# Seven rows of every four gathers, fetched by SyncE one at a time

## The chip, the cores and the metric

The kernel runs on 1 core of one Trainium2 chip. The metric is the device time of one execution in microseconds (us); the figure quoted is the median of three executions. A profile of one more execution gives the span from its first to its last instruction.

## The reference, cut to what matters

The reference is one layer of a graph network over 6250 nodes (128 features: 32 scalars and 32 vectors of three components) and 200,000 edges, sorted by receiving node (`dst`).

```python
h = relu(layernorm(x))                       # nodes
s, v = h[:, :32] @ W_up_s, h[:, 32:] x W_up_v  # the node table, 128 numbers a node
w = silu(silu(edge_feats @ A1 + b1) @ A2 + b2) @ A3   # 4 x 32 weights an edge
ss, vs = s[src], v[src]                      # one gathered row of the table an edge
out_s0 = ss * y_s * w0
out_s3 = sum_i(vs_i * y_v_i) / sqrt(3) * w3
out_v1 = ss * y_v * w1
out_v2 = vs * y_s * w2
message = segment_sum(concat(...), dst) / 10
out = x + (message x W_out)
```

## The kernel before

**First stage.** TensorE, ScalarE, VectorE and GpSimd compute the node table, 6272 rows of 512 bytes, in about 40 us, and SyncE stores it to HBM (`node_table`). Semaphore `table_stored` says that it is there.

**Edge stage.** The edges are padded and cut into tiles of 128 edges, one edge on each partition. Four tiles are a quad, four quads (16 tiles) a block, two blocks one iteration of the loop. There are NJ = 49 iterations; the last is written out after the loop and has fewer tiles. So a loop of 48 iterations does 96 blocks, or 384 quads, and the last iteration the rest (1563 tiles in all).

- **GpSimd (POOL), lines 519 to 543.** `gather(j, p)` waits, at the first quad of a block, for the block's sender numbers (`src_loaded`), then for the rows slot of the quad to be free (`msgs_ready`: the quad that used the slot one iteration ago has been consumed), and issues four indirect DMAs. Each reads 128 sender numbers, one on each partition of `src_in`, and fetches 128 rows of the table into `rows`. All four raise `gathered[p]`. There are eight slots, one for each quad of an iteration.
- **TensorE** computes the edge weights in three layers and, in `scatter`, multiplies each quad's messages by a one-hot matrix to sum them by receiving node in windows of 32 nodes.
- **VectorE** waits in `messages(j, p)` for `gathered[p]`, for the edge weights and for a messages slot, and multiplies rows by weights (lines 653 and 655). It also makes the one-hot matrices and adds the finished windows (`add_window`, which loads the window's start, one number, from SBUF into a register, line 663).
- **SyncE (SP), lines 482 to 515,** loads the inputs of blocks. In the loop, for each of the two blocks: it waits until the last quad of the block has been gathered, issues the load of the sender numbers of the same block of the next iteration (`load_src`, line 495), waits for layer 1 (`l1_done`), issues the edge features (line 486), waits for the one-hot matrices (`onehot_ready`), and issues the edge attributes and receivers (lines 491 and 492). Everything on SP runs in the order in which it is written.

The order of work on each engine is the order of the program; engines meet at semaphores alone.

Of the kernel before, what the change touches and what calls it, by code (L numbers as in the profile page):

```python
# [22 lines left out]
F32, I32 = mybir.dt.float32, mybir.dt.int32  # L23
ALU, ACT, AX = mybir.AluOpType, mybir.ActivationFunctionType, mybir.AxisListType

P = 128
# [6 lines left out]
NPAD = NT * P  # L33
CT = 7
NCH = NT // CT
PIECES = [(0, 4), (4, 3)]

GROUP = 2 * P
QT = 4
QUADS = 4  # L40
OW = QT
TILES = QT * QUADS
BLOCK = TILES * P
BODY = 2
QB = BODY * QUADS
NJ = -(-N_EDGES // (BLOCK * BODY))
NB = NJ * BODY
# [4 lines left out]
GP = 112  # L52
XW = NPAD + W
MAX_ROUNDS = NPAD // W + 1
SLOTS = 2
MSG_SLOTS = 4
HOT_SLOTS = 4
# [23 lines left out]
def quad_tiles(p):  # L81

    o, half = divmod(p, 2)
    begins = [o * OCT_EDGES + w * GROUP + half * P for w in range(OW)]
    return sum(b < LAST_EDGES for b in begins)


def gnn_layer_kernel(nc, x, xT, src, dst, dst_groups, attr, efT, Wus, Wuv, A1, b1, A2, b2, A3, Wos, Wov, outT):
    table = nc.dram_tensor("node_table", (NPAD, F), F32, kind="Internal").ap()
# [4 lines left out]
    with ctx:  # L94
        def sb(name, shape, dt=F32):
            return ctx.enter_context(nc.sbuf_tensor(name, shape, dt))
# [4 lines left out]
        def sem(name):  # L101
            return ctx.enter_context(nc.semaphore(name))
# [35 lines left out]
        rows = sb("rows", [P, QT * QB, F])  # L138
# [7 lines left out]
        ef_in = sb("ef_in", [2 * EF, BODY, 2 * MLP_HALF])  # L146
        attr_in = sb("attr_in", [P, BODY, TILES * 4])
        dst_in = sb("dst_in", [P, BODY, TILES], I32)
        src_in = sb("src_in", [P, BODY, TILES], I32)

        x_sb = sb("x_sb", [P, NT, F])
        tab_sb = sb("tab_sb", [P, NT, F])
# [37 lines left out]
        table_stored = sem("table_stored")  # L190
# [7 lines left out]
        round_step = sem("round_step")  # L198
        ef_loaded = [sem(f"ef_loaded{b}") for b in range(BODY)]
        attr_loaded = [sem(f"attr_loaded{b}") for b in range(BODY)]  # L200
        src_loaded = [sem(f"src_loaded{b}") for b in range(BODY)]
        gathered = [sem(f"gathered{p}") for p in range(QB)]
        src_again = sem("src_again")
        slots_claimed = sem("slots_claimed")
        l1_done = sem("l1_done")
        h1_ready = sem("h1_ready")
        l2_done = sem("l2_done")
        h2_ready = sem("h2_ready")
        w_ready = sem("w_ready")
        msgs_ready = sem("msgs_ready")  # L210
# [9 lines left out]

        out_stored = sem("out_stored")

        round_sems = [round_step, *ef_loaded, *attr_loaded, *src_loaded, *gathered, src_again, slots_claimed, l1_done, h1_ready, l2_done,
                      h2_ready, w_ready, msgs_ready, rel_ready, eq_ready, onehot_ready, scatter_done, sums_copied, sums_turned, turned_copied, out_ready,
                      window_added]

# [1 line left out]
        with nc.Block() as block:  # L228
# [154 lines left out]
            def _(dve):  # L383
# [28 lines left out]
                def count_rounds():  # L412
# [8 lines left out]
                    dve.wait_ge(rounds_step, 4)  # L421
                    dve.tensor_scalar(rounds_sb[:, :], span_windows[:, :], 1.0, float(MAX_ROUNDS),
                                      ALU.add, ALU.min).then_inc(rounds_step, 1)
# [56 lines left out]
        with nc.Fori(0, rounds):  # L480
            with nc.Block() as block:

                @block.sync
                def _(sp):
                    def load_ef(j, b):
                        sp.dma_start(ef_in[:, b, :], efT[bass.ds(j * BODY + b, 1), :, :].rearrange("a p n -> (a p) n")
                                     ).then_inc(ef_loaded[b], 16)

                    def load_attr(j, b):
                        n = bass.ds(j * BODY + b, 1)  # L490
                        sp.dma_start(attr_in[:, b, :], attr[n, :, :].rearrange("a p n -> (a p) n")).then_inc(attr_loaded[b], 16)
                        sp.dma_start(dst_in[:, b, :], dst[n, :, :].rearrange("a p n -> (a p) n")).then_inc(attr_loaded[b], 16)

                    def load_src(j, b):
                        sp.dma_start(src_in[:, b, :], src[bass.ds(j * BODY + b, 1), :, :].rearrange("a p n -> (a p) n")
                                     ).then_inc(src_loaded[b], 16)

                    for b in range(BODY):
                        sp.sem_inc(src_loaded[b], SRC_CREDIT)
                    for b in range(BODY):  # L500
                        load_ef(0, b)
                        load_attr(0, b)
                    with sp.Fori(0, NJ - 1) as j:
                        for b in range(BODY):
                            sp.wait_ge(gathered[b * QUADS + QUADS - 1], j * 16 * QT + 16 * QT)
                            load_src(j + 1, b)
                            sp.wait_ge(l1_done, j * 2 * BODY + 2 * b + 2)
                            load_ef(j + 1, b)
                            sp.wait_ge(onehot_ready, j * 2 * BODY + 2 * b + 2)
                            load_attr(j + 1, b)  # L510
                    for p in range(QB):
                        sp.wait_ge(gathered[p], (NJ - 1) * 16 * QT + 16 * quad_tiles(p))
                    for b in range(BODY):
                        sp.dma_start(src_in[:, b, :], src[b, :, :]).then_inc(src_again, 16)
                    sp.wait_ge(src_again, 16 * BODY)

                @block.gpsimd
                def _(pool):
                    pool.wait_ge(table_stored, 16 * NCH * len(PIECES))

                    def gather(j, p, tiles=QT):
                        b, k = divmod(p, QUADS)
                        if k == 0:
                            pool.wait_ge(src_loaded[b], j * 16 + 16)
                        pool.wait_ge(msgs_ready, j * QB + p + 1)  # L525

                        pool.sem_inc(slots_claimed, 1)  # L527
                        for t in range(tiles):
                            at = QT * k + t
                            pool.indirect_dma_start(  # L530
                                out=rows[:, QT * p + t, :], out_offset=None, in_=table,
                                in_offset=bass.IndirectOffsetOnAxis(ap=src_in[:, b, at:at + 1], axis=0),
                            ).then_inc(gathered[p], 16)

                    with pool.Fori(0, NJ - 1) as j:  # L535
                        for p in range(QB):
                            gather(j, p)

                    for p in range(QB):
                        gather(NJ - 1, p, quad_tiles(p))  # L540
                    for p in range(QB):
                        pool.wait_ge(gathered[p], (NJ - 1) * 16 * QT + 16 * quad_tiles(p))

                    pool.dma_reset()
# [60 lines left out]
                def _(dve):  # L605
# [36 lines left out]
                            .unsqueeze(3).broadcast_to([P, HT, 4, W]),  # L642
                            ALU.mult).then_inc(onehot_ready, 1)

                    def messages(j, p, tiles):

                        dve.wait_ge(gathered[p], j * 16 * QT + 16 * tiles)
                        dve.wait_ge(w_ready, j * QB + p + 1 + W_CREDIT)
                        dve.wait_ge(scatter_done, j * QB + p + 1)
                        g = rows[:, QT * p:QT * (p + 1), :].rearrange("p t (c u) -> p t c u", c=4)  # L650
                        m = msgs[:, p % MSG_SLOTS].rearrange("p t k (c u) -> p t k c u", c=4)
                        w = psw[:, p % SLOTS]
                        dve.tensor_tensor(m[:, :, :, 0, :], g[:, :, 0, :].unsqueeze(2).broadcast_to([P, QT, 2, MUL]),  # L653
                                          w[:, :, :, 0, :], ALU.mult)
                        dve.tensor_tensor(m[:, :, :, 1:4, :],  # L655
                                          g[:, :, 1:4, :].unsqueeze(2).broadcast_to([P, QT, 2, 3, MUL]),
                                          w[:, :, :, 1, :].unsqueeze(3).broadcast_to([P, QT, 2, 3, MUL]),
                                          ALU.mult).then_inc(msgs_ready, 1)
# [14 lines left out]
                    def iteration(j, first=False, last=False):  # L673
                        for p in range(QB):


                            g = p // 2 + 1
                            ahead = (j + g // 4, g % 4) if not (last and 2 * g >= QB) else None
                            n = 2 * p - WINDOW_LAG
                            if p % 2 == 0 and not (first and n < 0):  # L680
                                for i in range(OW):
                                    add_window(j, n + i)
                            messages(j, p, quad_tiles(p) if last else QT)
                            if ahead and p % 2 == 0:
                                relative(*ahead)
                                equal(*ahead)
                            elif ahead:
                                scale(*ahead)
# [5 lines left out]
                    with dve.Fori(1, NJ - 1) as j:  # L694
                        iteration(j)
# [164 lines left out]
```

## Time and profile before

| | us |
|---|---|
| time, median of 3 executions | 2016.88 (2015.19 to 2016.98) |
| time of the profiled execution | 2015.93 |
| its span, first to last instruction | 2014.1 |
| POOL busy | 1491.1 |
| TensorE matmuls busy | 1544.4 |
| VectorE busy | 977.5 |
| ScalarE busy | 418.5 |

The profile does not count instructions of an engine's queue as busy: register arithmetic, semaphores, branches and the issuing of DMAs by SP are shown with a q behind the engine's name (SPq, DVEq). Idle time that ends with "issue" is time in which the engine waited for nothing that the profile shows.

### The profile page before, as it was taken

How to read it: one execution, taken by the hardware profiler on the slowest of the kernel's cores; microseconds unless marked ns; L12 is line 12 of the kernel's file. 1: busy time of each engine (PE TensorE's matmuls, PEld its weight loads, DVE VectorE, ACT ScalarE, POOL GpSimd, SP SyncE). 2: the span in 40 equal slices, each digit the busy share in tenths (PEclk: the TensorE clock that was granted, in tenths of full speed). 3: DMA queues.
4: the chain of work that ended last, by engine and by line, in shares of the span. 5: the costliest groups of instructions: out<-in, count | busy, mean ns of one | idle time of the engine just before them, and what ended most of it. 6: DMA issues, size and time to landing. Idle time of an engine off the chain costs nothing.

```text
span 2014.1 us, 47833 instructions
## 1 busy us (share of the span) xinstructions
PE 1544.4 (77%) x16198; PEld 942.1 (47%) x16198; DVE 977.5 (49%) x2232; ACT 418.5 (21%) x836; POOL 1491.1 (74%) x1627
## 2 busy tenths in 40 slices
PE   6887787886877778868768787787777887776875
PEld 3444454454544545535445455454444454444543
DVE  4444444444444444444444444444444444444443
ACT  4222222222221222222222122222222222222121
POOL 4777777777777777777777777777777777777774
PEclk8888889789888897898898878988889789789787
DMA  8222222222222222222222222222222222222222
GB/s 230 58 61 57 59 58 59 57 60 57 59 58 59 57 60 58 57 60 57 59 58 59 57 60 57 59 58 59 57 60 57 59 58 59 57 60 57 59 58 100
DMA packets 111252, 128.24 MB, mean 64 GB/s; under 512 B 70786, under 2 KB 83362, under 8 KB 111108
## 3 DMA queue, kind: packets, MB, share of 16 engines
q0 software_dynamic: 50336, 102.64, 19.7%
q1 hardware_dynamic: 60324, 25.34, 4.8%
q8 instruction: 9, 0.15, 0.0%
q10 hardware_dynamic: 576, 0.05, 0.0%
q14 instruction: 7, 0.06, 0.0%
HBM read 121.47 MB, written 6.43 MB: 64 GB/s over the span
## 4 chain that ended last, share of the span: by engine, by line
POOL 71%; issue 25%; POOLq 1%; DMA 1%; PE 1%; SPq 1%; DVE 0%; ACT 0%; DVEq 0%; ACTq 0%
POOL rows L530 71%; DMA x_sb<-in_x 1%; POOLq L525 1%; POOLq L527 0%; POOLq L535 0%; SPq L246 0%; DMA node_table<-tab_sb 0%; SPq L236 0%; PE pss L750 0%; DVE bn L388 0%; DMA rows<-node_table,src_in 0%; PE psw L728 0%; DVE group_stats L439 0%; PE psw L456 0%; SPq L240 0%
## 5 line engine op out<-in xcount | busy, mean ns | idle before, releaser
L530 POOL DMA_INDIRECT rows<-node_table,src_in x1563 | 1475.3, 944 | 486.6 <-issue 486.6
L750 PE MATMUL pss<-msgs,onehot 128*32 128x64 f32 (+1 forms) x12544 | 336.1, 254 | 432.2 <-DVE msgs L655 430.6
L750 PEld LDWEIGHTS pss<-msgs,onehot 128*32 128x32 f32 x12544 | 264.3, 120 | 676.4 <-DVE msgs L655 659.3
L728 PE MATMUL psw<-a_bd,h 128*128 128x256 f32 x1568 | 564.4, 494 | 3.4
L653 DVE TENSOR_TENSOR msgs<-rows,psw 128x256 f32<-128x256 f32 x392 | 165.0, 421 | 797.6 <-DMA rows<-node_table,src_in 787.6
L655 DVE TENSOR_TENSOR msgs<-rows,psw 128x768 f32<-128x768 f32 x392 | 371.3, 947 | 0.0
L728 PEld LDWEIGHTS psw<-a_bd,h 128*128 128x128 f32 x1568 | 326.8, 231 | 86.2 <-issue 25.9
L565 ACT ACTIVATE h<-ps,b_sb 128x512 f32<-128x512 f32 x196 | 134.8, 688 | 996.7 <-PE ps L718 996.7
L712 PE MATMUL ps<-ef_in,a_bd 16*128 16x512 f32 x392 | 241.7, 698 | 12.1 <-DMA ef_in<-in_efT 10.4
L718 PE MATMUL ps<-h,a_bd 128*128 128x512 f32 x392 | 246.5, 716 | 0.9 <-ACT h L565 0.9
L671 DVE TENSOR_TENSOR xT_sb<-xT_sb,psx 128x32 f32 x784 | 145.9, 186 | 199.9 <-DVE xT_sb L671 157.3
L638 DVE TENSOR_TENSOR onehot<-psx,attr_in 128x1024 f32<-128x1024 f32 x196 | 238.7, 1218 | 0.0
L558 ACT ACTIVATE h<-ps,b_sb 128x512 f32<-128x512 f32 x196 | 134.7, 687 | 370.0 <-PE ps L712 370.0
L769 PEld LDWEIGHTS psx<-sums_t,w_out 128*128 128x128 f32 x784 | 168.9, 265 | 25.8 <-ACT sums_t L577 0.7
L769 PE MATMUL psx<-sums_t,w_out 128*128 128x128 f32 x784 | 161.0, 343 | 0.5 <-ACT sums_t L577 0.5
L761 PEld LDWEIGHTS psx<-identity,sums 128*128 128x128 f32 x392 | 41.4, 148 | 166.2 <-DVE xT_sb L671 89.4
L571 ACT ACTIVATE sums<-pss 128x256 f32<-128x256 f32 x196 | 75.3, 384 | 187.5 <-PE pss L750 164.0
L712 PEld LDWEIGHTS ps<-ef_in,a_bd 16*128 16x128 f32 x392 | 62.4, 198 | 86.8 <-issue 76.0
L761 PE MATMUL psx<-identity,sums 128*128 128x128 f32 x392 | 91.2, 317 | 1.9 <-ACT sums L571 1.1
L629 DVE TENSOR_TENSOR psx<-psx,rel 128x256 f32<-128x256 f32 x196 | 84.7, 432 | 6.8
L718 PEld LDWEIGHTS ps<-h,a_bd 128*128 128x128 f32 x392 | 78.6, 248 | 4.0 <-issue 3.9
L577 ACT ACTIVATE sums_t<-psx 128x256 f32<-128x256 f32 x196 | 73.9, 377 | 4.9 <-PE psx L761 4.9
(60 smaller groups left out, 138.5 us busy)
## 6 DMA issues: line engine op xcount, KB each, us to landing
rows<-node_table,src_in POOLq DMA_INDIRECT x1563
ef_in<-in_efT SPq DMA_DIRECT2D x98, 64.0 KB
xT_sb<-in_xT SPq DMA_DIRECT2D x7, 448.0 KB, 8.2
x_sb<-in_x SPq DMA_DIRECT2D x7, 448.0 KB, 7.4
attr_in<-in_attr SPq DMA_DIRECT2D x98, 32.0 KB
out_T<-xT_sb SPq DMA_DIRECT2D x1, 3136.0 KB, 8.8
node_table<-tab_sb SPq DMA_DIRECT2D x7, 256.0 KB, 3.9
src_in<-in_src SPq DMA_DIRECT2D x100, 8.0 KB, 1.6
```

The source lines that it names most:

```text
L530: pool.indirect_dma_start(out=rows[:, QT * p + t, :], out_offset=None, in_=table, in_offset=bass.IndirectOffsetOnAxis(ap=src_in[:, b, at:a ...
L558: act.activation(h1[:, o % 2, :], ps1[:, 0, :], ACT.Silu, bias=b1_sb[:, 0:1]).then_inc(h1_ready, 1)
L565: act.activation(h2[:, b, h, :], ps2[:, 0, :], ACT.Silu, bias=b2_sb[:, 0:1]).then_inc(h2_ready, 1)
L638: dve.tensor_tensor(onehot[:, g, :, :, :], eq.unsqueeze(2).broadcast_to([P, HT, 4, W]), attr_in[:, b, h * 4 * HT:(h + 1) * 4 * HT].rearran ...
L653: dve.tensor_tensor(m[:, :, :, 0, :], g[:, :, 0, :].unsqueeze(2).broadcast_to([P, QT, 2, MUL]), w[:, :, :, 0, :], ALU.mult)
L655: dve.tensor_tensor(m[:, :, :, 1:4, :], g[:, :, 1:4, :].unsqueeze(2).broadcast_to([P, QT, 2, 3, MUL]), w[:, :, :, 1, :].unsqueeze(3).broad ...
L671: dve.tensor_tensor(at, at, pso[:, i * W:(i + 1) * W], ALU.add).then_inc(window_added, 1)
L712: nc.tensor.matmul(ps1[:, 0, :], a1_bd[:, :], ef_in[:, b, h * MLP_HALF:(h + 1) * MLP_HALF], start=True, stop=True).then_inc(l1_done, 1)
L718: nc.tensor.matmul(ps2[:, 0, :], a2_bd[:, :], h1[:, o % 2, :], start=True, stop=True).then_inc(l2_done, 1)
L728: last = nc.tensor.matmul(psw[:, p % SLOTS, 2 * i:2 * i + 2].rearrange("p b c d e -> p (b c d e)"), h2[:, b, h, (2 * half + i) * P:(2 * ha ...
L750: last = nc.tensor.matmul(to, onehot[:, o, QT * half + w, c, :], moving, start=(half == 0 and c == 0), stop=(half == 1 and c == 3), skip_g ...
L769: last = nc.tensor.matmul(pso, w_out[:, k, :], sums_t[:, o % 2, k, :], start=(k == 0), stop=(k == 1))
```

## The change

GpSimd's four gathers of a quad fetch 128, 127, 126 and 124 rows, always from partition 0 on. The seven rows left over (one, two and four, on the last partitions) are fetched by SyncE, one plain DMA of 512 bytes each, whose source address comes from a register. For this the host appends the 28 sender numbers of a block's left-over edges to `src_in` (44 columns on each partition where there were 16), and SyncE loads the 28 numbers from partition 0 into registers at the head of each block, then waits at each quad for its slot. VectorE's `messages` waits for the seven single rows as well. The first wait of SyncE on the table (`table_stored`) is new. The last iteration, outside the loop, gathers full tiles as before.

```diff
+GATHER_ROWS = [P, P - 1, P - 2, P - 4]
+LEFT_OVER = [(t, e) for t, n in enumerate(GATHER_ROWS) for e in range(n, P)]
+SINGLES = len(LEFT_OVER)
+SRC_COLS = TILES + QUADS * SINGLES
...
-        src_in = sb("src_in", [P, BODY, TILES], I32)
+        src_in = sb("src_in", [P, BODY, SRC_COLS], I32)
...
+                    def gather_singles(j, b):
+
+                        sp.wait_ge(src_loaded[b], j * 16 + 16)
+                        sp.sem_inc(singles_claimed, 1)
+                        nodes = nc.values_load_multi_w_load_instructions(
+                            src_in[0:1, b, TILES:SRC_COLS], engines=[mybir.EngineType.SP], min_val=0, max_val=NPAD - 1,
+                            skip_runtime_bounds_check_because="the senders are node numbers")[1]
+                        for k in range(QUADS):
+                            p = b * QUADS + k
+                            sp.wait_ge(msgs_ready, j * QB + p + 1)
+                            sp.sem_inc(singles_claimed, 1)
+                            for (t, e), node in zip(LEFT_OVER, nodes[k * SINGLES:(k + 1) * SINGLES]):
+                                sp.dma_start(rows[e:e + 1, QT * p + t, :], table[bass.ds(node, 1), :]
+                                             ).then_inc(singles_gathered[p], 16)
+
...
+                    sp.wait_ge(table_stored, 16 * NCH * len(PIECES))
                     with sp.Fori(0, NJ - 1) as j:
                         for b in range(BODY):
+                            gather_singles(j, b)
                             sp.wait_ge(gathered[b * QUADS + QUADS - 1], j * 16 * QT + 16 * QT)
...
-                    def gather(j, p, tiles=QT):
+                    def gather(j, p, tiles=QT, last=False):
...
+                            n = P if last else GATHER_ROWS[t]
                             pool.indirect_dma_start(
-                                out=rows[:, QT * p + t, :], out_offset=None, in_=table,
-                                in_offset=bass.IndirectOffsetOnAxis(ap=src_in[:, b, at:at + 1], axis=0),
+                                out=rows[0:n, QT * p + t, :], out_offset=None, in_=table,
+                                in_offset=bass.IndirectOffsetOnAxis(ap=src_in[0:n, b, at:at + 1], axis=0),
                             ).then_inc(gathered[p], 16)
...
-                    def messages(j, p, tiles):
+                    def messages(j, p, tiles, last):
 
                         dve.wait_ge(gathered[p], j * 16 * QT + 16 * tiles)
+                        if not last:
+                            dve.wait_ge(singles_gathered[p], j * 16 * SINGLES + 16 * SINGLES)
```

## Rows read from the trace of the kernel before

**Rows 1.** The page: busy time by engine, and the chain that ended last by engine.
```profile
PE 1544.4 (77%) x16198; PEld 942.1 (47%) x16198; DVE 977.5 (49%) x2232; ACT 418.5 (21%) x836; POOL 1491.1 (74%) x1627
...
POOL 71%; issue 25%; POOLq 1%; DMA 1%; PE 1%; SPq 1%; DVE 0%; ACT 0%; DVEq 0%; ACTq 0%
```

**Rows 2.** The page's groups: instruction, count, busy us, mean ns, idle before, releaser.
```profile
L530 POOL DMA_INDIRECT rows<-node_table,src_in x1563 | 1475.3, 944 | 486.6 <-issue 486.6
...
L653 DVE TENSOR_TENSOR msgs<-rows,psw 128x256 f32<-128x256 f32 x392 | 165.0, 421 | 797.6 <-DMA rows<-node_table,src_in 787.6
```

**Rows 3.** Timeline of POOL from 1000 us: start us, duration us, what, idle before.
```profile
1001.70 0.94 POOL L530 DMA_INDIRECT rows<-node_table,src_in  x1 [0.30 <-issue]
1002.95 0.94 POOL L530 DMA_INDIRECT rows<-node_table,src_in  x1 [0.31 <-issue]
```

**Rows 4.** Waits of SP's queue: waiter, releaser, us in total, times, longest.
```profile
SPq L495 <- DMA rows<-node_table,src_in: 1690.3, 96, 21.0
```

**Rows 5.** Timeline of SP from 1003 us, one block to the next.
```profile
1003.17 0.33 SPq L495 DMA_DIRECT2D src_in<-in_src  x1
1003.79 0.33 SPq L486 DMA_DIRECT2D ef_in<-in_efT  x1
1004.31 0.33 SPq L491 DMA_DIRECT2D attr_in<-in_attr  x1
1004.87 0.33 SPq L492 DMA_DIRECT2D dst_in<-in_dst  x1
1023.14 0.33 SPq L495 DMA_DIRECT2D src_in<-in_src  x1
```

**Rows 6.** Timeline of SP near 32 us: loads to one partition, then one to 128.
```profile
31.92 0.29 SPq L256 DMA_DIRECT2D span_row<-window_spans  x1
32.25 0.23 SPq L257 DMA_DIRECT2D start_row<-window_starts  x1
32.53 0.35 SPq L258 DMA_DIRECT2D start_all<-window_starts  x1
```

**Rows 7.** SP's lines 486, 491, 503, 499: durations ns min/median/max, first and last start.
```profile
L486 SPq DMA_DIRECT2D ef_in<-in_efT x98: 331/331/429, 40.9 to 1962.7; - x98
L486 SPq FUSED_REGOPS  x96: 37/40/43, 65.4 to 1962.5; - x96
L486 SPq MOVE ef_in<-in_efT x96: 29/29/29, 65.5 to 1962.6; - x96
L491 SPq DMA_DIRECT2D attr_in<-in_attr x98: 332/336/423, 41.3 to 1963.2; - x98
L503 SPq MOVE  x1: 29/29/29, 43.7 to 43.7; - x1
L499 SPq EVENT_SEMAPHORE  x2: 17/17/17, 40.8 to 40.9; - x2
```

**Rows 8.** VectorE's queue, lines 663 and 694: register load of one number, register arithmetic.
```profile
L663 DVEq TENSOR_LOAD <-start_at x784: 297/303/330, 64.8 to 2003.2; - x196
L663 DVEq FUSED_REGOPS  x658: 46/55/71, 85.1 to 1955.4; - x165
L694 DVEq FUSED_REGOPS  x47: 98/98/104, 84.3 to 1922.5; - x47
```

**Rows 9.** Groups by line: plain DMAs issued by POOL, of 8 rows, then 64 rows.
```profile
L279 POOL DMA_DIRECT2D a_bd<-in_A x2 | 1.3, 656 | 0.1
L281 POOL DMA_DIRECT2D a_bd<-in_A x2 | 1.1, 551 | 0.0
```

**Rows 10.** The page: packets and bytes of the gathers' queue, share of 16 engines' span.
```profile
q0 software_dynamic: 50336, 102.64, 19.7%
```

**Rows 11.** Stretches of 20 us: PE, PEld, DVE, ACT, POOL busy, granted clock, DMA share, GB/s.
```profile
1000.00:1020.00 20.00, 12.81 (x178) 7.71 (x170) 9.73 (x22) 4.07 (x8) 15.12 (x17) 1.00 0.23 58
1040.00:1060.00 20.00, 17.20 (x172) 9.89 (x168) 9.75 (x23) 4.09 (x8) 15.12 (x17) 0.76 0.23 58
```

**Rows 12.** Timeline of the end: last load of senders, last gather, last window.
```profile
1962.03 0.33 SPq L495 DMA_DIRECT2D src_in<-in_src  x1
1993.06 0.94 POOL L530 DMA_INDIRECT rows<-node_table,src_in  x1 [0.30 <-issue]
2003.63 0.19 DVE L671 TENSOR_TENSOR xT_sb<-xT_sb,psx 128x32 f32 x1 [0.28 <-DVE xT_sb L671]
```

More of the change, by code:

```diff
@@ L203, in gnn_layer_kernel @@
         src_again = sem("src_again")
+        singles_gathered = [sem(f"singles_gathered{p}") for p in range(QB)]
         slots_claimed = sem("slots_claimed")
+        singles_claimed = sem("singles_claimed")
         l1_done = sem("l1_done")
@@ L221, in gnn_layer_kernel @@
         out_stored = sem("out_stored")
-        round_sems = [round_step, *ef_loaded, *attr_loaded, *src_loaded, *gathered, src_again, slots_claimed, l1_done, h1_ready, l2_done,
+        round_sems = [round_step, *ef_loaded, *attr_loaded, *src_loaded, *gathered, src_again, *singles_gathered, slots_claimed, singles_claimed, l1_done, h1_ready, l2_done,
                       h2_ready, w_ready, msgs_ready, rel_ready, eq_ready, onehot_ready, scatter_done, sums_copied, sums_turned, turned_copied, out_ready,
@@ L539, in _ @@
                     for p in range(QB):
-                        gather(NJ - 1, p, quad_tiles(p))
+                        gather(NJ - 1, p, quad_tiles(p), last=True)
                     for p in range(QB):
@@ L682, in iteration @@
                                     add_window(j, n + i)
-                            messages(j, p, quad_tiles(p) if last else QT)
+                            messages(j, p, quad_tiles(p) if last else QT, last)
                             if ahead and p % 2 == 0:
@@ L830 @@
     tiles = lambda a: np.ascontiguousarray(octs(a).reshape(NB, TILES, P, -1).transpose(0, 2, 1, 3).reshape(NB, P, -1))
+    senders = tiles(np.pad(src, (0, pad)))
+    singles = np.stack([senders[:, e, QT * k + t] for k in range(QUADS) for t, e in LEFT_OVER], axis=1)
     arrays = {
@@ L833 @@
         "xT": np.ascontiguousarray(x_pad[:, FEATURES].T),
-        "src": tiles(np.pad(src, (0, pad))),
+        "src": np.concatenate([senders, np.broadcast_to(singles[:, None, :], (NB, P, QUADS * SINGLES))], axis=2),
         "dst": tiles(dst_pad),
```

## The prediction

> **What bounds the kernel now.** I read the page's busy line and chain first. TensorE has the most busy time, but the chain that ended last is 71% POOL and 25% "issue" [rows 1], and the groups say that both are one line: 1563 gathers of 944 ns, with 486.6 us of "issue" between them, while VectorE's 797.6 us of idle time before the messages are ended by gathers landing [rows 2]. The timeline shows the pattern: a gather starts every 1.25 us, 0.94 of it busy and 0.30 between, whatever the other engines do [rows 3]. A block of 16 gathers so takes 19.97 us, the distance of SP's two `load_src` [rows 5]. The other engines have room: TensorE is busy for 12.8 to 17.2 us of a block (by its granted clock), VectorE for 9.7 [rows 11]. SP is nearly idle: it spends 1690.3 us waiting for gathers, 17.6 us in each of 96 blocks [rows 4]; its four loads of a block take 1003.17 to 1005.20 us [rows 5].
>
> So only two things in this change can move the time: what a gather costs POOL when it has a few rows less, and whether what SP gets to do fits in a block of 19.97 us.
>
> **POOL's side.** 96 blocks lose 28 rows each. The trace has only full gathers, so the price of a row is bounded. Above: if all 944 ns were per row, a row is 7.4 ns and a quad saves 52 ns, over 384 quads 20 us [rows 2]. At the other end: a plain DMA of 8 rows took POOL 656 ns and one of 64 rows 551 ns, so rows there cost nothing or less than nothing [rows 9]. I take zero, the nearest row about row counts, and keep -20 us. That a count that is no multiple of 16 makes a gather dearer can't be excluded by these rows (the 8-row DMA was the slower one, by 105 ns); three such gathers a quad at 105 ns more would be 0.32 us a quad, 121 us in all.
>
> **SP's side, by block.** What is added: 28 numbers loaded into registers, 28 DMAs each with its address arithmetic, five semaphore increments and five waits.
>
> *One single row.* A load with an address from a register is, on SP, a FUSED_REGOPS of 40 ns, a MOVE of 29 ns and the DMA instruction [rows 7]. The DMA instruction took 0.33 us for 16 or 128 partitions, with a register address or without [rows 5, 7]; the nearest to a single row is the load to one partition, 0.23 us when nothing was waited for [rows 6]. Between queue instructions lie about 0.04 us: 32.25 + 0.23 to 32.53 is 0.05 [rows 6]. Sum: (0.04 + 0.03 + 0.23) + 3 x 0.04 = 0.42 us; 28 of them 11.8 us. Bounds: 0.34 without the arithmetic (9.5 us) and 0.54 with a DMA of 0.33, two rounded gaps included (15.1 us).
>
> *The 28 register loads.* The trace has only a load of one number, on VectorE's queue: 303 ns [rows 8]. The low end is one instruction for all at the price of one, 0.35 us. The high end is one instruction, or its full price, for each: 28 x 0.34 = 9.5 us. I take the fixed part of an instruction off and pay the rest for each number, since the sequencer has to fetch each: register arithmetic there costs 55 to 98 ns [rows 8], which leaves 0.205 to 0.248 a number; with the mean, 28 x 0.226 + 0.08 = 6.4 us.
>
> The Trainium skill ("Runtime: NRT & Kernel Launch", section "Instruction fetch mechanics") says that a register load costs some 200 ns a register even in bulk. The 303 ns row, one register with its fixed part, agrees with that. By the page alone the 28 would be an estimated 5.6 us and the block 0.8 us shorter than below, an estimated 77 us less in all. It is the rule that speaks against this change: loading many numbers at once doesn't make them cheap.
>
> *The rest.* Five increments and up to five waits at 17 ns and a gap each [rows 7]: 0.6 us. The loads SP did before: 2.03 us, with the wait's own arithmetic ahead and half of the loop's branch some 2.4 us [rows 5, 7].
>
> Sum S = 11.8 + 6.4 + 0.6 + 2.4 = 21.2 us against 19.97. The bounds are 12.6 and 27.6.
>
> **What follows when S is over a block.** SP does everything in order. Behind the 28 DMAs stands `load_src` for the same block of the next iteration, and POOL's first gather there waits for it. While SP is early this wait is free: POOL needs the numbers one block later. When SP takes S > 20, POOL catches up with SP and waits for `src_loaded` at each block, and the period of the whole loop becomes S. The gathers' 4.97 us a quad stop being the bound.
>
> The total: SP's loop starts at 43.7 us [rows 7] and makes 96 turns; then come SP's last `load_src`, and behind it the 11 gathers of the final block (13.7 us), since POOL has by then finished the block before, the load's own issue and landing, some 2.3 us, and the 21.0 us from the last gather's start to the span's end [rows 12]. So span = 43.7 + 96 S + 37 = 81 + 96 S. At S = 21.2 it is 2116 us, and with the 1.8 us by which the profiled execution's time exceeds its span, 2118. The profiled execution was 1.0 us below the median. The change loses 102 us by this. It begins to lose at S = 20.1; below that the POOL path stands, as the wait before `load_src` had 17.6 us of room [rows 4].
>
> **What else is late, and doesn't decide.** SP starts the singles of a block only when the block before has been gathered. So VectorE's first quad of a block waits about 2.4 + 6.4 + 3 + 2 us, some 14 us, where gathers alone would let it go after 5 + 1.6; the quads behind come at 7 x 0.42 = 2.9 us. VectorE and TensorE catch up within the block (9.7 and at most 17.2 us of work [rows 11]), and the slot that POOL wants is eight quads, 40 us, old. No cost in the sum. The new waits on `msgs_ready` are met for the same reason; the wait for `table_stored` was POOL's anyway. `src_in` grows by 14 KB a block: nothing beside a queue at 19.7% [rows 10].
>
> **Rival 1, the SP work fits (S under 20.1): chance 0.30.** For it: the register load may be pipelined; two of the four terms have their low ends far down. The sum stays POOL's: 2016 less 0 to 20 us. Half of it or more would be faster by over 0.2%, if the rows cost anything. About 2008.
>
> **Rival 2, a gather of an odd count goes to few DMA engines or costs POOL more: chance 0.10.** The gathers' packets take 19.7% of 16 engines' span [rows 10], 0.197 x 16 x 2014 / 1563 = 4.06 us of one engine for a gather. Spread over 16 that is 0.25 us. If the 127-row gather went to one engine, it would take 4.0 us there, which lands about with the quad's last gather, issued 2.5 us later, and costs little as long as the engine changes from gather to gather. If it is always the same engine, 126 and 124 rows add their shares and seven singles theirs, up to 6.5 us a quad against 5.0: 2016 + 384 x 1.5 = 2590 us. It decides from 5.0 us a quad on.
>
> The Trainium skill ("DMA: Bandwidth & Descriptors", section "Why a DMA increments its semaphore by 16 and not by 1") says that the number of engines is the largest up to 16 that divides the partition count: 16 for 128, one for 127, 14 for 126, 4 for 124, and that GpSimd's choice goes round the engines. No row here shows it. With the round it makes landings later and leaves the time at the forecast.
>
> **Rival 3, dear register loads: inside the forecast's case.** If each number costs a whole instruction, S = 21.2 + 3.1 = 24.3 and the time is 2415 us. Against it only that one call loads a contiguous row.
>
> **Chances.** SP becomes the bound, at any price over 20.1: 0.60. Rival 1: 0.30, of which 0.18 faster and 0.12 within 0.2% (4 us, about what the measurement can tell from no change). Rival 2: 0.10, slower. Together faster 0.18, same 0.13, slower 0.69. The range takes in POOL's full saving (1996) and reaches to the dear register loads (2415); past it I leave the bound of 0.54 us a single with them, and the one-engine case.
>
> **What would show it.** SP's waits: the 1690.3 us before line 495's counterpart shrink to near nothing, and POOL shows waits on the load of `src_in` that it didn't have; `load_src` comes every S us instead of 19.97. SP's timeline prices each term: singles apart by 0.42 us, and the stretch without DMAs at a block's head is the register load. POOL's gathers, group by group of rows, show 944 ns for all or not. If SP still waits for gathers by more than a microsecond a block, the forecast is wrong, and the gather's mean duration says by how much it is faster; if SP is the bound but S isn't 21.2, a term is mis-sized and the timeline tells which.

## The result and the profile after

| | before | after |
|---|---|---|
| time, median of 4 executions, us | 2016.34 | 2787.47 |
| span of the profiled execution | 2014.1 | 2786.1 |
| POOL busy | 1491.1 | 2262.6 |
| SP's wait for gathers ahead of `load_src` | 1690.3 | 976.2 |

The change makes the kernel 1.38 times as slow (ratio 1.3824, 95% interval 1.38 to 1.3848). The forecast was 2118 us and its range ended at 2415. The direction came out right by luck: the loss has another cause than the forecast's, and another size.

The page of the changed kernel, its busy line, its chain and the two groups that answer to [rows 1, 2]:
```profile
PE 1763.3 (63%) x16198; PEld 1080.4 (39%) x16198; DVE 977.6 (35%) x2232; ACT 418.0 (15%) x836; POOL 2262.6 (81%) x1627
...
POOL 79%; issue 18%; POOLq 1%; DMA 1%; SPq 0%; PE 0%; DVE 0%; ACT 0%; DVEq 0%; ACTq 0%
...
L554 POOL DMA_INDIRECT rows<-node_table,src_in x1563 | 2246.7, 1437 | 486.5 <-issue 486.5
...
L679 DVE TENSOR_TENSOR msgs<-rows,psw 128x256 f32<-128x256 f32 x392 | 165.2, 421 | 1558.5 <-DMA rows<-node_table,src_in 1033.3
```
POOL's idle time ("issue") is what it was, 486.5 us. All of the loss is in the busy time of the gathers: 2246.7 - 1475.3 = 771.4 us, and the span grew by 772.0. The mean hides different durations, which the timeline shows. POOL in the changed kernel, from the start of one quad to the next, columns as in [rows 3]:
```profile
1002.98 0.98 POOL L554 DMA_INDIRECT rows<-node_table,src_in  x1 [0.30 <-issue]
1004.27 2.54 POOL L554 DMA_INDIRECT rows<-node_table,src_in  x1 [0.31 <-issue]
1007.11 0.99 POOL L554 DMA_INDIRECT rows<-node_table,src_in  x1 [0.30 <-issue]
1008.40 1.28 POOL L554 DMA_INDIRECT rows<-node_table,src_in  x1 [0.30 <-issue]
```
They are the gathers of 128, 127, 126 and 124 rows; the medians of the 384 at each position are 979, 2539, 979 and 1283 ns. The one with a single row less than before takes 2.7 times as long as before, while the one with four less takes half of that. Against 944 ns the four have 35 + 1595 + 35 + 339 = 2004 ns more, times 384 quads 770 us.

SP in the same kernel, answering to [rows 4, 5]: its waits, then its timeline over one block, then its register load of 28 numbers and its single-row DMA (min/median/max ns):
```profile
SPq L501 <- DMA rows<-node_table,src_in: 976.2, 96, 15.1
```
```profile
1027.13 0.36 SPq L501 DMA_DIRECT2D src_in<-in_src  x1
1027.78 0.32 SPq L492 DMA_DIRECT2D ef_in<-in_efT  x1
1028.28 0.35 SPq L497 DMA_DIRECT2D attr_in<-in_attr  x1
1028.82 0.80 SPq L498 DMA_DIRECT2D dst_in<-in_dst  x1
1032.21 12.79 SPq L516 DMA_DIRECT2D rows<-node_table  x28
1055.32 0.36 SPq L501 DMA_DIRECT2D src_in<-in_src  x1
```
```profile
L508 SPq TENSOR_LOAD <-src_in x96: 1659/1907/2591, 44.8 to 2710.4; - x96
...
L516 SPq DMA_DIRECT2D rows<-node_table x2688: 103/228/792, 46.8 to 2725.5; - x192
```
A block is now 28.2 us long (1027.13 to 1055.32), and SP is done with its part after 17.9 of them: it is not the bound, and waits 10.2 us a block.

### The profile page after: what moved, and what is told of

Same layout as the page of the kernel before. It is cut to its first block, busy times and chain, and to the rows that moved or that the text cites. A ratio compares the mean times of both kernels' runs of the same rounds, so it can differ in the third digit from the quotient of the medians.

```text
span 2786.1 us, 57385 instructions
## 1 busy us (share of the span) xinstructions
PE 1763.3 (63%) x16198; PEld 1080.4 (39%) x16198; DVE 977.6 (35%) x2232; ACT 418.0 (15%) x836; POOL 2262.6 (81%) x1627
## 3 DMA queue, kind: packets, MB, share of 16 engines
q0 software_dynamic: 167072, 104.79, 17.7%
## 4 chain that ended last, share of the span: by engine, by line
POOL 79%; issue 18%; POOLq 1%; DMA 1%; SPq 0%; PE 0%; DVE 0%; ACT 0%; DVEq 0%; ACTq 0%
POOL rows L554 78%; DMA x_sb<-in_x 0%; POOLq L548 0%; POOLq L550 0%; POOLq L559 0%; SPq L252 0%; SPq L242 0%; DMA node_table<-tab_sb 0%; DVE bn L394 0%; DMA rows<-node_table,src_in 0%; PE pss L776 0%; PE psw L754 0%; DVE group_stats L445 0%; ACT tab_sb L378 0%; SPq L246 0%
## 5 line engine op out<-in xcount | busy, mean ns | idle before, releaser
L554 POOL DMA_INDIRECT rows<-node_table,src_in x1563 | 2246.7, 1437 | 486.5 <-issue 486.5
L776 PE MATMUL pss<-msgs,onehot 128*32 128x64 f32 (+1 forms) x12544 | 398.4, 286 | 859.1 <-DVE msgs L681 858.8
L776 PEld LDWEIGHTS pss<-msgs,onehot 128*32 128x32 f32 x12544 | 314.1, 137 | 1134.2 <-DVE msgs L681 1093.6
L754 PE MATMUL psw<-a_bd,h 128*128 128x256 f32 x1568 | 651.2, 557 | 3.0 <-issue 0.2
L754 PEld LDWEIGHTS psw<-a_bd,h 128*128 128x128 f32 x1568 | 374.0, 264 | 105.8 <-issue 43.1
L738 PE MATMUL ps<-ef_in,a_bd 16*128 16x512 f32 x392 | 253.7, 731 | 135.9 <-DMA ef_in<-in_efT 134.5
L744 PE MATMUL ps<-h,a_bd 128*128 128x512 f32 x392 | 279.9, 806 | 0.9 <-ACT h L589 0.9
L795 PEld LDWEIGHTS psx<-sums_t,w_out 128*128 128x128 f32 x784 | 197.9, 308 | 34.0 <-ACT sums_t L601 0.7
L795 PE MATMUL psx<-sums_t,w_out 128*128 128x128 f32 x784 | 186.0, 384 | 0.5 <-ACT sums_t L601 0.5
L744 PEld LDWEIGHTS ps<-h,a_bd 128*128 128x128 f32 x392 | 90.7, 284 | 4.0 <-issue 3.9
```

Of the source, the lines that this page charges most:

```text
L554: pool.indirect_dma_start(out=rows[0:n, QT * p + t, :], out_offset=None, in_=table, in_offset=bass.IndirectOffsetOnAxis(ap=src_in[0:n, b, ...
L738: nc.tensor.matmul(ps1[:, 0, :], a1_bd[:, :], ef_in[:, b, h * MLP_HALF:(h + 1) * MLP_HALF], start=True, stop=True).then_inc(l1_done, 1)
L744: nc.tensor.matmul(ps2[:, 0, :], a2_bd[:, :], h1[:, o % 2, :], start=True, stop=True).then_inc(l2_done, 1)
L754: last = nc.tensor.matmul(psw[:, p % SLOTS, 2 * i:2 * i + 2].rearrange("p b c d e -> p (b c d e)"), h2[:, b, h, (2 * half + i) * P:(2 * ha ...
L776: last = nc.tensor.matmul(to, onehot[:, o, QT * half + w, c, :], moving, start=(half == 0 and c == 0), stop=(half == 1 and c == 3), skip_g ...
L795: last = nc.tensor.matmul(pso, w_out[:, k, :], sums_t[:, o % 2, k, :], start=(k == 0), stop=(k == 1))
```

## The experiments

In short: SP's half costs nothing, POOL's half costs all, and a gather's time on POOL goes by its share, the rows that its count leaves for one DMA engine: the count divided by its largest divisor up to 16. An experiment on SP's share and a faster version follow.

**SP's half alone.**
```diff
-        sp.dma_start(rows[e:e + 1, QT * p + t, :], table[bass.ds(node, 1), :]
+        sp.dma_start(spare[e:e + 1, p, t - 1, :], table[bass.ds(node, 1), :]
...
-        n = P if last else GATHER_ROWS[t]
+        n = P
```


> SP's half of the change alone: all gathers take 128 rows as before, and SP fetches the same 2688 single rows with the same register loads and waits, but into a tile of its own; VectorE still waits for them, nothing is left out. Theory A (the whole loss is POOL's gathers of uneven row counts; SP's 17.9 us a block fit in a block of 19.97): time within 5 us of the kernel before, 2011 to 2021 us, gathers of 944 ns, and SP still waits for gathers for 100 to 250 us in all. Theory B (SP's DMAs share something with POOL's and slow it, which would also be why the 128-row gather went from 944 to 979 ns): gathers of some 979 ns here, 2016 + 1536 x 0.035 = 2070 us. Theory C (SP is the bound once POOL is fast): 2050 us or more, with POOL waiting for src_in.

2016.2 us against 2015.4 (ratio 1.0004, interval 0.9994 to 1.0013): no difference. The group of POOL's gathers, SP's wait, and SP's timeline over a block:
```profile
L555 POOL DMA_INDIRECT rows<-node_table,src_in x1563 | 1478.7, 946 | 487.5 <-issue 483.2 <-DVE msgs L682 4.3
```
```profile
SPq L502 <- DMA rows<-node_table,src_in: 245.5, 73, 6.0
```
```profile
1004.78 0.36 SPq L502 DMA_DIRECT2D src_in<-in_src  x1
...
1009.47 11.98 SPq L517 DMA_DIRECT2D spare<-node_table  x28
1024.87 0.36 SPq L502 DMA_DIRECT2D src_in<-in_src  x1
```
The gathers take 946 ns beside 2688 more DMAs, 2 ns more than before and not the 35 of theory B, so B falls; SP still waits, so theory C falls. SP's work is 1009.47 + 11.98 - 1004.78 = 16.7 us a block.

**POOL's half alone.** The uneven gathers, without the single rows: those are not fetched, and their places in `rows` hold zeros, written once ahead of the loop. The three experiments behind this one have the same edit with other counts.
```diff
+        n = P if last else GATHER_ROWS[t]
-        out=rows[:, QT * p + t, :], ... ap=src_in[:, b, at:at + 1]
+        out=rows[0:n, QT * p + t, :], ... ap=src_in[0:n, b, at:at + 1]
```


> POOL's half alone: gathers of 128, 127, 126 and 124 rows, and the seven rows of a quad that are left over aren't fetched at all (their place holds zeros). Theory A: 2016 + 384 x 2.0 = 2785 us, the same four durations by position as in the changed kernel (979, 2539, 979, 1283 ns), the 128-row gather at 979 too if its extra 35 ns come from its neighbours. Theory B: durations shorter than in the changed kernel by what SP's DMAs add, the 128-row gather back at 944.

2786.55 us (ratio 1.3826, interval 1.3803 to 1.3849): the whole loss. POOL's timeline, from a gather of 127 rows to the next quad's of 128:
```profile
1003.13 2.54 POOL L533 DMA_INDIRECT rows<-node_table,src_in  x1 [0.30 <-issue]
1005.98 0.99 POOL L533 DMA_INDIRECT rows<-node_table,src_in  x1 [0.30 <-issue]
1007.27 1.28 POOL L533 DMA_INDIRECT rows<-node_table,src_in  x1 [0.30 <-issue]
1008.86 0.98 POOL L533 DMA_INDIRECT rows<-node_table,src_in  x1 [0.30 <-issue]
```
The four durations are those of the changed kernel, the 0.98 of the full gather among them: SP had no part in that one either.

**Other divisors.** The four gathers with 112, 120, 121 and 113 rows.

> Four other row counts for the gathers of a quad: 112, 120, 121, 113; the rows left over aren't fetched. Theory A (POOL's time is 0.88 us + 13.1 ns for each row of the fullest engine, and the rows are split over the largest number of engines up to 16 that divides the count): 112 on 16 engines, 7 each, 0.97 us; 120 on 15, 8 each, 0.98; 121 on 11, 11 each, 1.02; 113 on one, 113 each, 2.36; in all 2016 + 384 x 1.5 = 2610 us. Rival D (the price is for each row missing from 128, or for any count that is no multiple of 16): 112 cheap, 113, 120 and 121 all alike, with 121 near 113.

2607.9 us against an expected 2610 (ratio 1.2939). POOL's timeline, from a gather of 112 rows:
```profile
1004.01 0.94 POOL L533 DMA_INDIRECT rows<-node_table,src_in  x1 [0.30 <-DVE msgs L658]
1005.25 0.98 POOL L533 DMA_INDIRECT rows<-node_table,src_in  x1 [0.30 <-issue]
1006.54 1.02 POOL L533 DMA_INDIRECT rows<-node_table,src_in  x1 [0.30 <-issue]
1007.86 2.37 POOL L533 DMA_INDIRECT rows<-node_table,src_in  x1 [0.30 <-issue]
```
113 rows, a prime, take 2.37 us and 121 = 11 x 11 take 1.02. Rival D, a price for each row missing or for any count that is no multiple of 16, is out: 112 rows, with 16 missing, cost least of the four, and 121 and 113 would be near each other.

**Multiples of 16.** The gathers with 128, 96, 64 and 32 rows.

> Row counts that are multiples of 16: 128, 96, 64, 32; the rows left over aren't fetched. Theory A with its slope: 8, 6, 4 and 2 rows an engine, so 944, 918, 892 and 866 ns, a quad 156 ns shorter, 2016 - 60 = 1956 us. Rival E (the time of a gather goes by its rows, 7.4 ns each): 944, 708, 472, 236 ns, a quad 1.4 us shorter, and TensorE or VectorE the bound near 1600 us.

1969.6 us (ratio 0.9773). POOL's timeline, a quad:
```profile
1002.18 0.96 POOL L533 DMA_INDIRECT rows<-node_table,src_in  x1 [0.30 <-issue]
1003.44 0.92 POOL L533 DMA_INDIRECT rows<-node_table,src_in  x1 [0.30 <-issue]
1004.67 0.91 POOL L533 DMA_INDIRECT rows<-node_table,src_in  x1 [0.30 <-issue]
1005.88 0.87 POOL L533 DMA_INDIRECT rows<-node_table,src_in  x1 [0.30 <-issue]
```
A quarter of the rows costs 873 ns where all cost 952 (medians), so rival E is out: 37% of the kernel's gathered rows, left away, bring 46 us. (952 - 873) / 6 is 13.2 ns for each row of an engine's share. The 1956 us expected were 14 too few, since the full gather took 952 here and not 944 and the others 4, 18 and 7 more than expected.

**The same share from three counts.** The gathers with 128, 31, 62 and 124 rows.

> Gathers of 128, 31, 62 and 124 rows; the rows left over aren't fetched. 31 rows divide over one engine, 62 over two, 124 over four: 31 rows an engine in each. If POOL's time goes by the share of the fullest engine, all three take the 1283 ns that 124 rows took, a quad is 3 x 0.34 us longer, and the time 2016 + 384 x 1.03 = 2412 us. If it goes by the rows in all, or by rows and engines separately, 31 rows take clearly less than 124.

2402.9 us against an expected 2412 (ratio 1.1924). POOL's timeline, 31, 62, 124 and 128 rows:
```profile
1004.30 1.26 POOL L533 DMA_INDIRECT rows<-node_table,src_in  x1 [0.31 <-issue]
1005.87 1.27 POOL L533 DMA_INDIRECT rows<-node_table,src_in  x1 [0.30 <-issue]
1007.44 1.28 POOL L533 DMA_INDIRECT rows<-node_table,src_in  x1 [0.30 <-issue]
1009.02 0.98 POOL L533 DMA_INDIRECT rows<-node_table,src_in  x1 [0.30 <-issue]
```
This is the sharpest of them: 31 rows cost within 2% of 124 (1257 and 1280 ns) and more than 128 (977). The share decides, not the count.

**What the packets show.** The queue of the gathers, packets and bytes: the changed kernel, then the multiples of 16, then this run.
```profile
q0 software_dynamic: 167072, 104.79, 17.7%
q0 software_dynamic: 50336, 64.89, 13.4%
q0 software_dynamic: 105632, 71.76, 13.6%
```
The multiples of 16 have the 50,336 packets of the kernel before [rows 10], with fewer bytes. The changed kernel has 3.3 times as many with 2% more bytes, and this run 2.1 times as many with fewer bytes. The sizes of the single packets in the traces tell why. A packet holds at most 8 rows (4096 bytes). The counts of each size fit 16 equal parts for a gather of 128 rows, 14 for 126 (packets of 8 rows and of 1), 11 for 121 (8 and 3), 4 for 124 (three of 8, and 7), 2 for 62, and one part for 31, 113 and 127: 127 rows are 15 packets of 8 rows and one of 7.

The parts that are missing to 16 have packets too, with 4 bytes for each row of the share: for 127 rows, 15 times 508 bytes. They are 263 packets of 32 bytes and 27 of 28 a quad in the changed kernel, where the kernel before has none of these sizes. So the queue gets 16 parts as long as the share, whatever the number of rows. That POOL's time is the time of writing them is the likely reading, not a shown one. It is not the time of moving the rows: in the changed kernel the gather of 127 rows that starts at 1004.27 us is over for POOL at 1006.81, and its first packet starts at 1007.48.

**All seven rows off one gather.** The whole change, with its seven single rows, but from the fourth gather alone.
```diff
-GATHER_ROWS = [P, P - 1, P - 2, P - 4]
+GATHER_ROWS = [P, P, P, P - 7]
```


> The whole change with the seven rows of a quad all taken from the fourth gather: 128, 128, 128 and 121 rows. By the share of the fullest engine (121 rows on 11 engines, 11 each) the fourth gather costs 1024 ns and the others 944: 2016 + 384 x 0.08 = 2047 us; if each full gather near an uneven one costs 979, as the one in the changed kernel did, 2087 us. If instead the loss came from the number of rows that SP fetches, or from SP at all, the time stays near 2787 us.

2052.9 us against 2015.1 (ratio 1.0191, interval 1.0174 to 1.0208). POOL's timeline, a quad:
```profile
1004.20 0.98 POOL L554 DMA_INDIRECT rows<-node_table,src_in  x1 [0.30 <-issue]
1005.48 0.94 POOL L554 DMA_INDIRECT rows<-node_table,src_in  x1 [0.31 <-issue]
1006.73 0.94 POOL L554 DMA_INDIRECT rows<-node_table,src_in  x1 [0.30 <-issue]
1007.97 1.01 POOL L554 DMA_INDIRECT rows<-node_table,src_in  x1 [0.30 <-issue]
```
With the same rows moved to SP, the loss is 38 us in place of 771. The 121 rows take 1007 ns, and of the full gathers only the one that follows them takes 977; 384 x (0.063 + 0.033) = 37 us. Between my two expectations: one gather pays for an uneven neighbour, not three.

**More work for SP.** SP's half alone, with the first two quads of a block fetched twice.
```diff
+        for again in range(2 if k < 2 else 1):
+            sp.dma_start(spare[e:e + 1, again, p, t - 1, :], table[bass.ds(node, 1), :]
```


> SP alone as before (all gathers of 128 rows, single rows into a tile of their own), but the first two quads of a block fetch their seven rows twice: 42 DMAs a block where there were 28. SP then has 16.7 + 14 x 0.42 = 22.6 us of work a block. By the forecast's own formula SP is now the bound and the span is 81 + 96 x 22.6 = 2250 us, with POOL waiting for the senders' numbers. If something else hides SP's work, the time stays at 2016 us.

2125.1 us (ratio 1.0545, interval 1.0524 to 1.0566). POOL's waits, and SP's timeline over a block:
```profile
POOL rows L556 <- DVE msgs L684: 79.4, 56, 1.9
POOL rows L556 <- DMA src_in<-in_src: 39.2, 28, 2.0
```
```profile
1019.21 0.36 SPq L502 DMA_DIRECT2D src_in<-in_src  x1
...
1023.88 16.52 SPq L518 DMA_DIRECT2D spare<-node_table  x42
1040.71 0.36 SPq L502 DMA_DIRECT2D src_in<-in_src  x1
```
```profile
L518 SPq DMA_DIRECT2D spare<-node_table x4032: 143/228/330, 44.8 to 2080.6; - x192
L518 SPq FUSED_REGOPS  x2688: 37/37/125, 44.7 to 2080.5; - x192
```
This block is 21.5 us long, the distance of two `load_src` (21.2 is the mean), and POOL now has waits at the head of blocks, for the senders' numbers, that neither the kernel before nor the changed one has (the trace puts 56 of the 84 down to VectorE). The expected 2250 us were too many, since the 14 added DMAs lengthen SP's stretch by 16.52 - 11.98 = 4.54 us, 0.32 each and not 0.42: a row fetched twice has its address arithmetic once (2688 for 4032 DMAs). S is then 16.7 + 4.5 = 21.2 us, for which the forecast's 81 + 96 S gives 2116; the span is 2123.3. So the forecast's mechanism exists. SP's work of 17.9 us a block does not reach it; from where on it sets in, between that and 21.2 us, was not measured.

**A faster version.** All gathers keep 128 rows, and SP takes a whole tile in 64 off POOL: 32 rows a block, over four blocks, into a ninth slot of `rows`. GpSimd's and SP's loops are two iterations long, VectorE's too, so that which quad has the ninth slot is fixed in the code.
```diff
-        rows = sb("rows", [P, QT * QB, F])
+        rows = sb("rows", [P, QT * (QB + 1), F])
...
+        if odd and p == LAST_QUAD:
+            tiles = QT - 1
...
+        for m, node in enumerate(nodes):
+            sp.dma_start(rows[e0 + m:e0 + m + 1, QT * QB + QT - 1, :], table[bass.ds(node, 1), :]
+                         ).then_inc(singles_gathered, 16)
```


> A version built on what the runs showed: every gather keeps 128 rows, and SP takes one whole tile in 64 off POOL, 32 rows a block over four blocks, into a ninth rows slot. POOL has 24 gathers of 1.25 us less: 2016 - 30 = 1986 us, if SP's work of some 16.7 + 4 x 0.43 + 0.2 = 18.6 us a block stays under the 19.67 us that a block then takes. If SP's work is over that, 2016 us or more.

1985.28 us against 2015.13 (ratio 0.9853, interval 0.9837 to 0.9869), 30 us or 1.5% less. Its gathers' group, SP's wait, SP's timeline and its register load of 32 numbers:
```profile
L569 POOL DMA_INDIRECT rows<-node_table,src_in x1539 | 1452.4, 944 | 477.8 <-issue 476.9 <-DVE msgs L699 0.6 <-DMA rows<-node_table,src_in 0.3
```
```profile
SPq L512 <- DMA rows<-node_table,src_in: 92.4, 73, 4.5
```
```profile
1027.98 0.36 SPq L512 DMA_DIRECT2D src_in<-in_src  x1
...
1032.43 13.38 SPq L528 DMA_DIRECT2D rows<-node_table  x32
1047.96 0.36 SPq L512 DMA_DIRECT2D src_in<-in_src  x1
```
```profile
L521 SPq TENSOR_LOAD <-src_in x96: 1895/2042/2066, 43.6 to 1915.4; - x96
```
24 gathers less at 944 + 304 ns are 30.0 us. SP's wait is down to 1 us a block, so SP has hardly more to give in this way.

## Why the prediction was wrong

**What bounds the kernel: right before, wrong after.** POOL's gathers set the time before and after, with the same "issue" beside them; the forecast had SP take over. SP still waits 10.2 us a block for gathers, which the prediction had named as the sign that its forecast is wrong.

**The step that failed: "I take zero, the nearest row about row counts, and keep -20 us."** I priced POOL's side of the change at -20 to 0 us, with 121 us as what could not be excluded, from a plain DMA of 8 rows at 656 ns and one of 64 at 551 [rows 9]. The measured term is +770 us. The two plain DMAs were of the wrong kind: both counts leave few rows to an engine (1 and 4, if the same rule holds for them), so they could not show what a share of 31 or 127 costs. My bounds came from the number of rows; the time goes by the share. The medians: shares of 2, 4 and 6 rows took 873, 910 and 922 ns; shares of 7, 8 and 9 rows 944 to 984; 11 rows 1007 to 1024; 31 rows 1257 to 1283; 113 rows 2367; 127 rows 2539. From 31 to 127 that is 13.1 ns a row.

**Rival 2 had half of it.** It placed the loss in an uneven gather going to few engines, and its heading names a higher cost on POOL, but it priced the DMA engines' time (4.0 us for one gather, hidden if the engine changes) and left POOL's own time as it was. The Trainium skill ("DMA: Bandwidth & Descriptors", section "Why a DMA increments its semaphore by 16 and not by 1") gives the rule by which the runs' durations sort: 16, 1, 14 and 4 engines for 128, 127, 126 and 124 rows. The prediction quotes the rule. What I concluded from it, "leaves the time at the forecast", was wrong, because I took the number of engines to matter for the moving of the data alone. The packets bear out the division, part by part; which engines the parts went to, the traces do not say. Whether always the same engine is loaded could not show in the time either: POOL takes 7.0 us a quad by itself, longer than the 6.5 us of that rival. Nor do that rival's own terms reach 6.5: 127 + 31 + 9 + 8 rows at 4.06 us for 128 are 5.6 us, and a single row's packet took 27 ns.

**SP as the bound: wrong, by its size.** I had S = 21.2 us of work a block; it is 16.7 (17.9 in the changed kernel, where some single DMAs take up to 0.79 us and the load of the receivers 0.80). The single rows were right: 0.43 us each by 11.98 / 28 against 0.42. The register load was not: 28 numbers in one instruction took 1.81 us in the SP-alone run and 1.91 in the changed kernel, where I had 6.4. One number is 303 ns on VectorE's queue [rows 8], so the further ones cost some 60 ns each; the 32 numbers of the faster version took 2.04 us, 58 ns for each of the four more. The Trainium skill ("Runtime: NRT & Kernel Launch", section "Instruction fetch mechanics") puts a register at about 200 ns even in bulk, which would be an estimated 5.6 us; for this load, from SBUF, the measurement goes against it. I had leaned on the row's fixed part and on nothing that tells a first number from a second. With 1.9 in place of 6.4 my own sum gives 16.7, under the 20.1 at which I said that SP begins to matter; the run with more work for SP shows that it does matter at 21.2. (The low bound of S adds up to 12.9 us, not 12.6; nothing rests on it.)

**The rest.** The latency steps (singles late at the head of a block, VectorE and TensorE catching up) cost nothing, as forecast: VectorE waits for singles in the SP-alone run, and the time stays. Rival 1's first half, that SP's work fits, came true; its conclusion, about 2008 us, failed with POOL's term.

## What to carry to other kernels

Keep the row count of an indirect gather at a multiple of 16, or at least where its largest divisor up to 16 leaves a small share; a large prime such as 127 is the worst case: here one row less made a gather 2.7 times as long. Where a gather is nearly all fixed cost (873 ns for 32 rows, 944 for 128, and 304 between two), taking rows off it brings little; taking whole gathers off does more, and an idle queue that can issue a row in 0.4 us can carry some of them. When a mean duration jumps, look at the instructions one by one before explaining it.

## What the runs showed of the hardware that was not expected

- GpSimd's time for an indirect gather of 512-byte rows is 0.84 to 0.89 us plus 13 ns for each row of the share, and the share is the count divided by its largest divisor up to 16: 31, 62 and 124 rows cost 1257, 1272 and 1280 ns.
- A gather that goes to fewer than 16 parts puts packets for the missing parts into the queue too, with 4 bytes for each row of the share: 167,072 packets in the changed kernel against 50,336 before.
- A gather of 128 rows behind one of 124 or 121 takes 977 to 979 ns and not 944, with SP's DMAs or without, and behind one of 32 rows 952. What it does in this time is open; a gather of 112 rows behind one of 113 took 944.
- One register load of 28 numbers from SBUF took SP 1.81 us (median; 1.91 in the changed kernel), one of 32 numbers 2.04.
- A plain load of one row of 512 bytes with its address in a register takes 228 ns of SP's queue in itself, and 0.42 to 0.46 us with its address arithmetic and the gaps (13.38 / 32 and 12.79 / 28); without the arithmetic, for a row fetched again, 0.32.
